# Another order of the steps of attention and recurrence on each engine, in a two-layer transformer kernel

## The reference, cut to what matters

```python
x = x + ln(attention(ln(x)))       # 16 heads, a window of 128 tokens, plus 4 "latent" heads over 64 pooled tokens, a gate, a projection
x = x + ln(ffn_ternary(ln(x)))     # 256 -> 1024 -> gelu -> 256, ternary weights
x = x + ln(rwkv(ln(x)))            # r, k, v, w projections; then a recurrence over time:
#   bonus = exp(u + k_t) v_t ;  o_t = r_t (s + bonus) ;  s = w_t s + k_t v_t
#   o is normalised per head of 16, scaled, shifted, multiplied by r, projected
x = x + ln(experts(ln(x)))         # 16 experts of width 128, top 4, plus a shared one
```

## Time and profile before

| what | value |
|---|---|
| median of 3 runs | 2587.27 us (2584.97 to 2589.25) |
| profiled execution, its own time | 2582.47 us |
| span in the profile | 2580.7 us |
| loop of 7 passes | 242.7 to 1686.4 us of the span |
| one pass, from the third on | 206.6 to 208.4 us |
| expert layer | from about 1855 us |

### The profile page before, as it was taken

The page is one execution under the profiler, slowest core; times in us unless marked ns, Lnnn a source line. Parts: engine busy times, 40 slices in busy tenths (PEclk is TensorE's granted clock), DMA queues, the critical chain, the costliest instruction groups (busy, mean ns, idle before and its releaser), DMA issues. The chain is left out here.

```text
span 2580.7 us, 31081 instructions
## 1 busy us (share of the span) xinstructions
PE 2159.6 (84%) x11049; PEld 1341.9 (52%) x11152; DVE 1637.6 (63%) x2846; ACT 840.8 (33%) x1530; POOL 607.1 (24%) x357
## 2 busy tenths in 40 slices
PE   0878987997997897888898798855279999999998
PEld 0544544554554454554454455422157777777775
DVE  3235796696696597588679669658355555555553
ACT  0342442352343333434344235310133222222222
POOL 0000242243143043133224214314111120112010
PEclk9779999899898998999999989875589999999999
DMA  4000000000000000000000000000210000000000
GB/s 121 1 1 9 1 1 18 1 2 17 1 1 9 10 1 9 10 1 1 18 1 1 18 1 1 1 8 0 65 55 19 17 17 17 0 17 16 16 1 17
DMA packets 32303, 33.46 MB, mean 13 GB/s; under 512 B 4496, under 2 KB 31184, under 8 KB 31952
## 3 DMA queue, kind: packets, MB, share of 16 engines
q1 hardware_dynamic: 32144, 31.38, 4.0%
HBM read 22.99 MB, written 8.39 MB: 12 GB/s over the span
## 5 line engine op out<-in xcount | busy, mean ns | idle before, releaser
L557 DVE TENSOR_TENSOR_SCAN s_buf<-r_work,kvb 128x512 f32<-128x512 f32 x256 | 366.3, 1431 | 0.0
L655 POOL TENSOR_TENSOR p_buf<-s_buf,r_work 128x512 f32<-128x512 f32 x128 | 151.7, 1185 | 486.7 <-DVE s_buf L557 486.7
L1563 PE MATMUL mbank<-m_xh,w_hi 128*128 128x512 f32 x544 | 228.7, 420 | 0.0
L1371 DVE TENSOR_TENSOR hl<-hf,hh 128x512 fp32r<-128x512 f32 x136 | 93.9, 691 | 199.8 <-ACT hh L1478 199.2
L710 ACT ACTIVATE probs<-bank_s,nmx 128x256 f32<-128x256 f32 (+1 forms) x512 | 186.5, 450 | 103.4 <-DVE nmx L420 99.8
L655 POOL TENSOR_TENSOR r_work<-s_buf,r_work 128x512 f32<-128x512 f32 x128 | 164.9, 1288 | 234.8 <-DVE s_buf L557 234.8
L1563 PE MATMUL mbank<-m_xl,w_hi 128*128 128x512 f32 x544 | 215.5, 396 | 0.0
L1563 PE MATMUL mbank<-m_xh,w_lo 128*128 128x512 f32 x544 | 215.5, 396 | 0.0
L728 ACT ACTIVATE pt<-bank_s 128x1024 f32<-128x1024 f32 (+1 forms) x128 | 117.5, 918 | 240.7 <-PE bank_s L988 240.7
L1474 ACT ACTIVATE sg<-mbank 128x512 f32<-128x512 f32 x136 | 81.2, 597 | 325.7 <-PE mbank L1563 325.6
L546 DVE TENSOR_TENSOR kvb<-r_work,bank 128x512 f32<-128x512 f32 x256 | 174.2, 681 | 16.2 <-PE bank L1106 5.4
(11 more groups left out here) (251 smaller groups left out, 4231.4 us busy)
## 6 DMA issues: line engine op xcount, KB each, us to landing
w_raw<-in_w SPq DMA_DIRECT2D x17, 256.0 KB, 2.8
x_new<-in_x SPq DMA_DIRECT2D x8, 512.0 KB, 3.5
x_after_rwkv<-x_b SPq DMA_DIRECT2D x8, 512.0 KB, 3.5
m_x_tok<-x_after_rwkv SPq DMA_DIRECT2D x8, 512.0 KB, 3.8
out<-m_x_tok SPq DMA_DIRECT2D x8, 512.0 KB, 2.9
w_raw<-in_w2e SPq DMA_DIRECT2D x17, 128.0 KB, 2.7
work<-in_w SPq DMA_DIRECT2D x2, 1024.0 KB
wrk<-in_wrk SPq DMA_DIRECT2D x1, 1024.0 KB
```

What stands on the lines that cost most here:

```text
L557: V.tensor_tensor_scan(s_buf[:, n % 2, 1:S + 1], dec[:, n // HD, :], kvb[:, n % 2, :], 0.0, ALU.mult, ALU.add).then_inc(sem["state"], 1)
L655: G.tensor_tensor(p_slot(n), s_buf[:, n % 2, 0:S], rf[:, n // HD, :], ALU.mult).then_inc(sem["rs"], 1)
L1563: ins = T.matmul(o, w[:, e, cols:cols + P], m, start=first and c == 0, stop=last and c == 2)
```

## The change: four other strings

Nothing but the four strings is changed; every instruction of every engine is the same, and only its place in its own engine's stream may differ.

```diff
 ORDER = dict(
-    tensor="araarrrrarrrararrararrarararrararrararrarrarraraarrararraararrarararararaaarrraarrararraaaarrarrraaraaraaaaaraa",
-    vector="arararrrrarrraaraarrrrrararararrararrararrarraararrararrararraararrarararaaararrararrrrarararaaarraaraaraaaaaraa",
-    scalar="aarrrrrarrraarrarraraaarraraarrrrraaaaarrrraraararraaaarrraarrrarraraararrrrraaaararrrarrrrraaararaaraaaraaaa",
-    gpsimd="arararrarrraaaarrrarrraarrrrrraararrraaararaarrrrararaaaaaraarraararrrrrarrarraaaaraaarrrrraarrrarrraaraaaaaraa",
+    tensor="aaarrarrrrrrararrarrraraararraararrarrarararrraararararrraarrarararrraararaaraaarrrrrraarrrrraaaaarraaaaraaraaaaa",
+    vector="ararrrarrarrraararrrrraraarraararrarararraarrarararrarraarrarararraarraraarrarararaarrrrarraararraaaaraaraaaaaraa",
+    scalar="aarrrrrraarrraarrraraaarrraraararrrrarrrrrararrrarraaraaraaaarrrraaarraaaaraararaarrarrarrrarrrraaaarraaaaaaarraa",
+    gpsimd="arrrrrarrarrrarrrrrraraarrarararrrrarrrarraararrarraaraaaraaaarraarraraararraaaaaarraaraaarraarrrrarraraararaa",
 )
```

More of the change, by code:

```diff
@@ L60 @@
 ORDER = dict(
-    tensor="araarrrrarrrararrararrarararrararrararrarrarraraarrararraararrarararararaaarrraarrararraaaarrarrraaraaraaaaaraa",
-    vector="arararrrrarrraaraarrrrrararararrararrararrarraararrararraararraraarrararaaararrararrrrarararaaarraaraaraaaaaraa",
-    scalar="aarrrrrarrraarrarraararaarraraarrrrraaaaarrrraraararraaaarrraarrrarraraararrrrraaaararrrarrrrraaararaaraaaraaaa",
-    gpsimd="arararrarrraaaarrrarrraarrrrrraararrraaararaarrrrararaaaaaraarraararrrrrarrarraaaaraaarrrrraarrrarrraaraaaaaraa",
+    tensor="aaarrarrrrrrararrarrraararraararrarrarararrraararararrraarrarararrraararaaraaarrrrrraarrrrraaaaarraaaaraaraaaaa",
+    vector="ararrrarrarrraararrrrraarraarararrarararraarrarararrarraarrararraarraraarrarararaarrrrarraararraaaaraaraaaaaraa",
+    scalar="aarrrrrraarrarrraraaarrraraararrrrarrrrrararrraarraaraaraaarrrraaarraaaaaraarararrarrarrrarrrraaaarraaaaaaarraa",
+    gpsimd="arrrrrarrarrrarrrrrraraarrarararrrarrrarraararrarraaraaaaraaaraarrraaararraraaaaaarraaraaaarraarrrrarraraararaa",
 )
```

## The result

| what | before | after |
|---|---|---|
| median, us | 2587.27 (7 runs, 2583.51 to 2591.01) | 2562.84 (7 runs, 2560.12 to 2574.61) |
| ratio, 95% interval | | 0.9911, 0.9893 to 0.9929 |
| profiled execution, its own time, us | 2582.47 | 2564.95 |
| its span, us | 2580.7 | 2563.1 |

A forecast was written before the change was run, and what follows sets the result against it. VectorE was taken to set the pace in the scan stage, TensorE in the feed-forward, with no engine full between. Terms: -4.6 + 4.7 = +0.1 us a pass, 7 x 0.1 = +0.7, giving 2588 us; range 2566 to 2608.

The forecast's parts named there:

- ScalarE's `k` and GpSimd's `scores0`: ScalarE's four k copies ahead of the projections and GpSimd's 3.3 us product moved behind scan14: each taken as 0.
- The rest of the scan stage: VectorE after the eighth kv: 1.3 us less waiting for scores, 1.5 less from stretched scans, 0.4 lost at scan17.
- From the last scan to the mixture: Scan 31 and the addition come earlier, so TensorE takes the mixture sooner; gain 4.6 us a pass, bounds 2.4 and 5.4.
- The feed-forward: o_norm and o_back moved earlier: TensorE idles 3.7 us, ffn4 starts 3.3 late, low clock costs 1.4; loss 4.7 us a pass.
- the 0.2 at the start: Start of the scans: eighth kv 0.2 us earlier; first-scores wait goes, remote's grows 1.1, a 0.5 spread-row wait comes.
- the start of the scans gains as well: Rival, faster: the waits for remote and the first scores, 3.9 us, both go; 2561 us, chance 0.07.

The follow-up runs named there:

- sc_gp_only: Kernel before with ScalarE's and GpSimd's new strings alone; 2581.08 us, ratio 0.9999.
- start_pe: Kernel before with TensorE's three swaps at the start of the scans alone (lat_turn1 behind scan1, scan4 ahead of remote, scores0 ahead of scan5); 2574.04 us, 0.9930.
- before_scan: Kernel before with the scan-stage part alone: new order of TensorE and VectorE up to scan 30 and GpSimd's new string; 2550.37 us, 0.9858.
- best_nodum: Changed kernel with o_norm and o_back back in their old places and without the 18 dummy products of mix; 2552.05 us, 0.9877.
- back12: Kernel before with 12 in place of 8 dummy products ahead of o_back's transposes, no order changed; 2579.20 us, 0.9961.
- back20: Kernel before with 20 in place of 8 dummy products ahead of o_back's transposes, no order changed; 2588.37 us, 1.0005.
- the singles: Kernel before with one TensorE swap each: lat_turn1 behind scan1 (0.9967), scan4 ahead of remote (0.9989), scores0 ahead of scan5 (1.0005).

## Why the prediction was wrong

- *ScalarE's `k` and GpSimd's `scores0`*: taken as 0, and `sc_gp_only` shows no difference (0.9999, 0.9969 to 1.0030; stretch B 27.3 in all).
- *The rest of the scan stage*: I took 2.4 us (1.3 for waits, 1.5 for fewer stretched scans, less 0.4). The scans gave the 1.5 exactly (44.8 to 43.3) and the waits for scores went; D shortened by 1.6, so some 0.8 came back elsewhere, at places that I did not all find: over the whole profile VectorE's idle time ahead of line 546 grew from 16.2 to 20.0 us, 0.5 a pass.
- *From the last scan to the mixture*: with the scan stage 4.6 us. Measured 1.6 + 3.2 = 4.8. The way was mine: the gain is TensorE's, while the mixture is ready 0.6 us later against scan 30. That the size held is partly luck, since two misses cancel: the scan stage gave 0.8 less than my 2.4, and the stretch behind scan 30 gave 1.2 more than the 2.0 that were left for it. I had the mixture 1.1 to 2.0 us later against scan 30 and not 0.6, and had subtracted up to 1.9 us for a low clock in the projection, where F grew by 0.1 alone.
- *The feed-forward*: 4.7 us, measured 5.3 in the profile and 5.0 in the medians. Line 593 waited 6.0 us (some 6 predicted), TensorE stood 3.4 (3.7), and the low clock behind the stop cost about 1.6 (1.4): eight products took 3.5 us instead of 1.8.
- *The step that failed* is the one at the start of the scans, the 0.2 us in "Together with the 0.2 at the start", and with it the silent one that everything outside my two places stays as it was. Instead of 0.2, stretch C gave 2.2 and stretch A, for which there was no term, 1.0. Together 3.2 us a pass; 7 x (3.2 - 0.2) = 21 of the 25 us by which I missed.

The other terms missed by 0.2 us a pass together, and the medians are 7 us further apart than the traces. The step that failed is worth a closer look. I walked the start through in pass 3 with durations as they stood, over half of the stretch at 1.2 GHz, and kept that clock for the new order. At the clock that I read the walk is right: pass 3 has 13.7 us of low clock in C and takes 25.61 us, and the three passes with the new start and as much of it (one each in `start_pe`, `before_scan` and `best_nodum`) take 25.44 to 25.48, with the wait for the scores gone and the one for `remote` 0.9 us longer.

What I had wrong is that the clock stays: in pass 5 TensorE's granted clock in C rose from 0.79 to 0.92, and on average 10.2 us at 1.2 GHz became 4.9.

The rival "the start of the scans gains as well" named the place and came out at nearly this time (2561 us). Of its two waits the one for the scores went in all seven passes (2.1 us on average); the one for `remote` fell only from 1.3 to 1.0. Both hang on the clock as well as on the order: in pass 1 of the kernel before, with 3.4 us of low clock, neither is over 0.2 us. At the same 10.2 us of low clock C takes 24.9 us before and 24.1 to 24.2 after, at 6.8 us 22.5 with the old start (`back12`) and 23.2 with the new one (`before_scan`), at 3.4 us 21.1 before (one pass) and 21.6 to 21.9 after. So the order by itself gives C nothing that is certain; less low clock gives it.

That this much can come and go with no step moved is shown by `back12` and `back20` (2.2 and 2.6 us a pass). How the 3.2 us divide between the new order of TensorE's start and the mere place of a pass against the clock stays open. So does which of the three swaps matters: no pair of them was run, and the singles were each profiled once.

## What to carry to other kernels

Look at the granted clock of each stretch in every pass of a loop before one pass is taken for all: where TensorE falls to the low level at the same places pass after pass, that pattern is a part of the time that a small shift can take away or bring, and other executions of the same kernel may not have it. On such a baseline parts measured singly may not add up, so measure a change also against a kernel that is only made longer by a known time. A walk through one pass holds for the clock of that pass: do it again with durations of a pass at the other level. And where an engine is late with dummy work in front of a waiting input, ask what released the dummies: moving that release may be worth more than the input.

## What the runs showed of the hardware that was not expected

- The same instructions in the same order took from 21.1 to 25.6 us within one execution (C in passes 1 and 2 of before, granted clock 0.92 and 0.73), and in pass 5 24.9 or 22.5 us depending on how long the pass was elsewhere (`back12`, 0.79 or 0.85). The Trainium skill (TensorE: Matmul & The Clock Gate, "What's actually happening") says that the monitor behind the clock runs freely and does not start over with the kernel; the runs agree in so far as a shift of 0.9 us in another stage changed where the low clock fell.
- Small operations pay for GpSimd as large ones do: line 430 (128x16) took 0.80 us, until GpSimd's second product ended (790.19), for 0.17 without; line 454 took 2.22 for 1.20, and of two products the one beside scan 31 took 2.09 us, the next 1.08 (3.15 together). That is the exclusive lock of the Trainium skill (SBUF — State Buffer, "SBUF: two separate sides") with the loser fully blocked, on either side.
